# A kernel of two cross attentions and four blocks: TensorE's bursts of identity products left out, and the first attention's shift rows sent in another place of SyncE's queue

## The reference, cut to what matters

```python
x = x + xattn(ctx, ln(x), ...)          # first cross attention, no mask
x = x + selective_scan(ln(x), ...)      # state-space scan, 256 channels x 16 states
x = x + experts(ln(x), ...)             # attention of 4 heads and 8 experts + a shared one
x = x + xattn(ctx, ln(x), mask, ...)    # second cross attention, context mask
x = x + state_space(ln(x), ...)         # 4 heads, convolution of 4, state 64
x = x + fp4_block(ln(x), ...)           # weights and inputs rounded to blocks of fp4

def xattn(x, latents, mask, ...):       # x: 1601 rows, latents: 64 rows
    xn, ll = layer_norm(x), layer_norm(latents)
    q = ll @ Wq
    k, v = split(concat([xn, ll]) @ Wkv)
    weight = softmax(q @ k.T * scale)   # 16 heads of 64
    return (weight @ v) @ Wo
```

## Time and profile before

| what | value |
|---|---|
| device time, median of 3 runs | 2011.71 us (2007.66 to 2015.58) |
| the profiled execution, its own time | 2016.63 us |
| its span | 2014.9 us |
| mean granted clock of TensorE | 0.972 |
| busy: TensorE, VectorE, ScalarE, GpSimd | 94%, 82%, 63%, 46% |
| first attention's loop: its first product | at 67.68 us |
| second attention's loop: its first product | at 1104.69 us |

### The profile page before, as it was taken

The page is one execution under the profiler, slowest core; times in us unless marked ns, Lnnn a source line. Parts: engine busy times, 40 slices in busy tenths (PEclk is TensorE's granted clock), DMA queues, the critical chain, the costliest instruction groups (busy, mean ns, idle before and its releaser), DMA issues. The chain is left out here.

```text
span 2014.9 us, 34833 instructions
## 1 busy us (share of the span) xinstructions
PE 1900.2 (94%) x12250; PEld 1028.9 (51%) x12250; DVE 1646.1 (82%) x3926; ACT 1266.2 (63%) x2267; POOL 921.5 (46%) x1016
## 2 busy tenths in 40 slices
PE   7899999999999999898888999999999999998786
PEld 6444545445454545433756445454545454545584
DVE  7789899888989896599686887979797878886657
ACT  4466667676767667444234887777777777776312
POOL 5576666676667652198432533323232323232004
PEclk9899999999999999989998999999999999999898
DMA  5223222222222120132203021112111111110000
GB/s 164 70 69 89 77 80 69 69 69 69 82 69 69 53 69 2 48 118 91 83 11 82 14 48 40 39 39 61 40 39 40 43 37 44 35 31 20 12 1 11
DMA packets 148711, 110.53 MB, mean 55 GB/s; under 512 B 120876, under 2 KB 136216, under 8 KB 148408
## 3 DMA queue, kind: packets, MB, share of 16 engines
q1 hardware_dynamic: 148536, 108.31, 19.5%
HBM read 65.15 MB, written 14.29 MB: 39 GB/s over the span
## 5 line engine op out<-in xcount | busy, mean ns | idle before, releaser
L1334 DVE TENSOR_TENSOR x_p_lo<-x_psum,x_p_hi 128x512 f16<-128x512 f32 (+1 forms) x864 | 581.2, 682 | 106.5 <-ACT x_psum L1086 106.4
L1085 ACT ACTIVATE x_p_hi<-x_psum 128x512 f16<-128x512 f32 (+1 forms) x448 | 268.1, 599 | 254.2 <-PE x_psum L925 207.0
L1085 ACT ACTIVATE x_p_hi<-x_psum,x_bcol 128x512 f16<-128x512 f32 (+1 forms) x416 | 289.1, 695 | 141.2 <-PE x_psum L925 138.2
L951 PE MATMUL x_psum<-x_p_hi,x_x_both 128*128 128x512 f16 (+1 forms) x832 | 317.4, 381 | 6.5 <-DVE x_p_lo L1334 5.6
L923 PE MATMUL x_psum<-x_q,x_xT_both 128*128 128x512 f16 x832 | 316.9, 381 | 6.7 <-DMA x_q<-x_shift_rows 6.7
L924 PE MATMUL x_psum<-x_q,x_xT_both 128*128 128x512 f16 x832 | 316.3, 380 | 0.0
L925 PE MATMUL x_psum<-x_q,x_xT_both 128*128 128x512 f16 x832 | 316.3, 380 | 0.0
L952 PE MATMUL x_psum<-x_p_lo,x_x_both 128*128 128x512 f16 (+1 forms) x832 | 315.9, 380 | 0.0
L953 PE MATMUL x_psum<-x_p_hi,x_x_both 128*128 128x512 f16 (+1 forms) x832 | 315.8, 380 | 0.0
L1273 DVE CUSTOM_DVE_ANT_0 x_junk<-x_psum,x_brow 128x512 bf16<-128x512 f32 (+2 forms) x512 | 279.3, 584 | 6.5 <-PE x_psum L1002 6.3
L1276 DVE TENSOR_REDUCE x_mx<-x_psum 128x1 f32<-128x512 f32 (+2 forms) x512 | 276.4, 583 | 3.3 <-PE x_psum L1002 2.9
(11 more groups left out here) (506 smaller groups left out, 3588.0 us busy)
## 6 DMA issues: line engine op xcount, KB each, us to landing
x_x_both<-context_rows SPq DMA_DIRECT2D x32, 832.0 KB, 5.1
context_rows<-x_x SPq DMA_DIRECT2D x16, 832.0 KB, 3.4
x_raw<-in_ctx SPq DMA_DIRECT2D x16, 768.0 KB
ssm_c_row<-ssm_bc_rows SPq DMA_DIRECT2D x16, 512.0 KB, 4.6
ssm_b_wide<-ssm_bc_rows SPq DMA_DIRECT2D x7, 512.0 KB, 3.6
x_mrow<-in_mask_BxS_bk SPq DMA_DIRECT2D x16, 200.1 KB
x_xT_both<-context_rows SPq DMA_TRANSPOSE x96, 3.9
moe_W<-in_L_ffn_eW SPq DMA_DIRECT2D x3, 512.0 KB, 5.6
```

The lines of the kernel that those rows point to most:

```text
L951: pe.matmul(out, v_hi, p_hi[r][rows, :], start=start, stop=False)
L1085: act.activation(p_hi[r][rows, :], score[r][rows, :], ACT.Exp, scale=SCORE_UNIT, **bias).then_inc(p_hi_ready, 1)
L1334: v.tensor_tensor(p_lo[r][rows, :], score[r][rows, :], p_hi[r][rows, :], ALU.subtract).then_inc(p_lo_ready, 1)
```

## The change

All 21 calls of `keep_clock` are left out, and the function with them. In the first attention SyncE's queue changes in two ways. The store of batch 0 is split: `store_high` writes the high half from inside the preparation as soon as GpSimd has cast it, and the front transpose of batch 0 follows there; `store_low` writes the low half at the start of the loop's block. And for batch 1 `rows_in` stands right behind the front transpose; the other transposes, the raw rows of batch 3 and the load of batch 1 come behind it. The second attention's queue is as it was.

```diff
-def keep_clock(pe, bank, ident, n):
-    for _ in range(n):
-        pe.matmul(bank[:, 0:P], ident[:, :], ident[:, :], start=True, stop=True)
...
+        def store_high(sp):
+            sp.wait_ge(x_hi_ready, 1)
+            sp.dma_start(kept(0)[:, 0, :, :], x16[:, 0, :, :]).then_inc(high_stored, 16)
+            sp.wait_ge(high_stored, 16)
+
+        def store_low(sp):
+            sp.wait_ge(x16_ready, 1)
+            sp.dma_start(kept(0)[:, 1, :, :], x16[:, 1, :, :]).then_inc(x_stored, 16)
+            sp.wait_ge(x_stored, 16)
...
                         load_raw(sp, 1, 1, 0)
+                        store_high(sp)
+                        load_xT_front(sp, 0, 0)
...
-                    keep_clock(pe, slot_psum[3], ident, 4 if loaded else 10)
                     pe.wait_ge(fold_ready, 1)
...
                     read(pe, N_PREP - 4)
-                    keep_clock(pe, slot_of(N_PREP), ident, 4)
...
                 if not masked:
-                    store_x(sp, 0)
-                    load_xT_front(sp, 0, 0)
+                    store_low(sp)
                     load_xT_rest(sp, 0, 0)
                     load_x(sp, 0, 0)
                 rows_out(at)
...
                     load_raw(sp, 2, 0, 1)
                     store_x(sp, 1)
+                    load_xT_front(sp, 1, 1)
+                rows_in(at)
+                if not masked:
+                    load_xT_rest(sp, 1, 1)
                     load_raw(sp, 3, 1, 1)
-                    load_xT_front(sp, 1, 1)
-                    load_xT_rest(sp, 1, 1)
                     load_x(sp, 1, 1)
-                rows_in(at)
...
                 if kind == "turn":
-                    if isinstance(at, Pre):
-                        keep_clock(pe, aux[:, 512:1024], ident, 7)
                     pe.wait_ge(m_ready, at.n + 1)
...
                     aux_item(at, item)
-                keep_clock(pe, acc[0], ident, 14)
                 for u in range(AHEAD):
                     scores(u, 0, 0, 0, 0)
...
-                keep_clock(pe, slot[1], ident, 12)
                 pe.wait_ge(in_in, 16)
...
-                keep_clock(pe, slot[1], ident, 6)
                 pe.wait_ge(rest_in, 48)
...
-                keep_clock(pe, slot[1], ident, 5)
                 pe.wait_ge(fold_ready, 1)
                 pe.wait_ge(xnT_ready, 1)
...
-                keep_clock(pe, slot[3], ident, 22)
                 pe.wait_ge(heads_in, HEADS_IN)
...
-                keep_clock(pe, slot[3], ident, 5)
                 pe.wait_ge(wt_ready, 1)
                 pe.wait_ge(nxT_ready, 1)
                 product(slot[2], WT[:, Q, :], nxT, q_made)
                 product(slot[3], WT[:, K4, :], nxT, k_made)
-                keep_clock(pe, slot[0], ident, 5)
...
-                keep_clock(pe, slot[1], ident, 8)
                 pe.wait_ge(uT_ready, GROUPS)
...
-                keep_clock(pe, slot[1], ident, 12)
                 pe.wait_ge(xf_ready, 1)
...
-                keep_clock(pe, slot[1], ident, 5)
                 pe.wait_ge(xf_hi_ready, 2)
...
-                keep_clock(pe, slot[3], ident, 24)
                 pe.wait_ge(matrices_in, MATRICES_IN)
...
-                keep_clock(pe, slot[3], ident, 5)
                 pe.wait_ge(wt_ready, 3)
                 pe.wait_ge(uT_ready, 1)
...
-                keep_clock(pe, slot[3], ident, 26)
                 pe.wait_ge(yn_ready, 1)
...
-                keep_clock(pe, slot[1], ident, 10)
                 pe.wait_ge(yg_ready, 2)
...
-                keep_clock(pe, slot[3], ident, 34)
                 turn(0)
-                keep_clock(pe, slot[3], ident, 3)
                 up(0)
```

More of the change, by code:

```diff
@@ L183, in cross_attention @@
         xT_front, xT_back, xT_low = ([sem(f"{n}{k}") for k in range(2)] for n in ("xT_front", "xT_back", "xT_low"))
-        x_stored, x_hi_ready = sem("x_stored"), sem("x_hi_ready")
+        x_stored, x_hi_ready, high_stored = sem("x_stored"), sem("x_hi_ready"), sem("high_stored")
         lat_crossed = sem("lat_crossed")
@@ L606, in attention_loop @@
     if not masked:
-        load_raw, store_x, halves = held["load_raw"], held["store_x"], held["halves"]
+        load_raw, store_x, store_low, halves = held["load_raw"], held["store_x"], held["store_low"], held["halves"]
         context_mean, context_guess = held["context_mean"], held["context_guess"]
```

## The result

The median is 2022.18 us (five runs, 2021.02 to 2026.12) against 2012.78 for the kernel before (five runs, 2007.66 to 2015.58): a ratio of 1.0058 with a 95% interval from 1.0039 to 1.0077, or +9.4 us. The forecast was 2019, +7.45 to the median shown then, within a range of 2009 to 2026. A second set of the same kernel (experiment 5) gave 1.0032, from 1.0020 to 1.0043, or +6.6 us. By either the change loses more than the shift rows gain; the centre of the second lies within 0.5%, that of the first just above. One execution in experiment 6, of 3292.91 us at a granted clock of 0.586, is left out of its comparison.

The account below looks back on a forecast made before the run. TensorE, busy for 94% of the span, was taken to bound the kernel, with cold clock restarts of 2.15 us on the mean. C to J lose 13.45, B gains 6.0: +7.45 on 2011.71 gives 2019 us, range 2009 to 2026.

Parts of the forecast that it names:

- D: Start of the expert stage: twelve transposes and the products behind them run cold, +3.15 us (0 to 4.6).
- E: Ahead of the experts: transposes at half speed and first expert products cold, +2.85 us (-0.3 to 4.2).
- G: Start of the second attention's loop: cold without its burst, +2.15 us (0.5 to 3.55).
- I: End of the state-space stage: last product starts cold after a pause, +2.15 us (0 to 3.55).
- C: Start of the scan stage: transposes start earlier but slower, input products start cold, +1.85 us (-0.3 to 3.25).
- H: Start of the state-space stage: a DMA sets the late end, product behind perhaps cold, +0.5 us (-0.4 to 1.75).
- J: Last stage: four cold transposes and a longer cold stretch, +0.8 us (0.3 to 1.5).
- A and B: First attention: preparation's later clock hides behind VectorE, 0; earlier shift rows start the loop at 61.4, -6.0 us.
- F: Second attention's preparation: products start as much earlier as they run longer cold, 0, ends one restart (2.15 us) either way.
- Long restarts: Rival: cold stretches of 7.1 us instead of 4.29 at C, D, E, G and I, 2027.4 us; chance 0.20.
- Warm pauses: Rival: work before each pause keeps the clock up at C, D, E, G and I, 2008.4 us; chance 0.13.
- the rows would come no earlier: Rival: the first attention's shift rows arrive no sooner, so B is 0 and the time 2025.2 us; chance 0.05.

Follow-up runs that it names:

- experiment 5: The changed kernel once more, nothing altered: 2020.96 us (nine runs) against 2014.36 for the kernel before, ratio 1.0032.
- experiment 6: The changed kernel with bursts put back at both attention loops' starts, 2015.05 us; then also in the expert stage and at the state-space stage's end, 2009.33; before 2014.36.
- experiment 2: The kernel before with all bursts gone and SyncE's queue left as it was: 2027.38 us against 2014.82, ratio 1.0060.
- the loops' run: The changed kernel with the bursts at the two attention loops' starts put back: 2015.05 us against 2014.36 for the kernel before, ratio 1.0003.
- experiment 3: The changed kernel with the six bursts of the expert stage put back: 2012.14 us against 2014.82 for the kernel before, ratio 0.9993.
- experiment 7: GpSimd waits for VectorE in the first preparation: changed kernel 2021.31 us, changed queue with all bursts 2004.40, that with four bursts fewer 2004.27; before 2012.99.
- four places: The changed kernel with bursts back at both loops' starts, the expert stage and the state-space stage's end: 2009.33 us against 2014.36 before, ratio 0.9976.
- experiment 7's third kernel: Changed queue, GpSimd's added wait, all bursts but four (state-space stage's start, last stage): 2004.27 us, ratio 0.9950 to the kernel before.
- single transposes: The kernel before with each identity product made one transpose of the identity: 2019.10 us against 2014.82, ratio 1.0022.
- the queue's second profile: Second run of the kernel before with only SyncE's queue changed and all bursts kept: 2002.13 us against 2012.99, ratio 0.9940.
- the queue with the wait: The kernel before with the changed SyncE queue, all bursts, and GpSimd waiting for VectorE in the first preparation: 2004.40 us, ratio 0.9945.
- experiment 4: The kernel before with each identity product made one transpose, 2019.10 us against 2014.82, or two transposes, 2014.42 against 2014.36.

## Why the prediction came out as it did

The forecast of 2019 was 3 us from the first median and 2 from the second, within its range. It held as a sum of two halves: 12.6 lost against 13.45, 3.2 or 6.0 gained against 6.0 (experiment 2). That the sum of the terms came out near is in part luck: in the first profile D, E, G and I cost 3.7 us more than forecast and the middle of the state-space stage 0.8, while C, H and J cost 5.8 less. C, D and J lie outside the bounds of their own terms. The terms, one by one:

**A and B.** Right. SyncE's queue moved as worked out, the store had landed at 56.81, VectorE was the last with 59.23, the rows took 2.04 to the first product, and this began at 61.30 for a forecast of 61.4. Two misses cancel in this: the rows left at 59.26 for 58.6, and took 2.04 for 2.8. That this start is cold in both kernels was right as well, but the restart cost 1.05, not 0.3: the clock rose at 67.2 here, 5.9 us behind the first product, and at 71.4 before, 3.7 behind it, and the lag goes from -6.38 to -5.33. It was given back behind that, in a stretch that the sum didn't have: at the end of the first batch the clock fell again, from 109.0 to 115.8 before and from 104.7 to 108.1 here, and the lag is -6.57 after it. The step that failed is the cover in A: VectorE was said to hide whatever the cold front of the preparation costs. VectorE's subtraction begins at 25.83 to 26.10 in the seven profiles with the first burst and at 25.83 to 26.66 in the seven without. That is enough that in two of the six without burst and wait (the second of the changed kernel, and the loops' run) GpSimd was first and VectorE took 2.5 us or more longer. (In a third, experiment 3, GpSimd's record begins 0.01 us ahead, and it was GpSimd that took longer.) It doesn't decide the median (experiment 7).

**C.** The size was +1.85 and the first profile has -0.83, the second +1.71 (137.99 - 136.28). The products without a burst were cold in four of the profiles (7.27 to 7.59 us: changed again, bursts gone alone, loops, four places) and warm, 5.51, in three (changed, its version with the wait, bursts in experts); with a burst they took 5.50 or 5.51 in all seven. So the mechanism was right, and whether it strikes differs from execution to execution: by these seven it does in some half of them, and the term should have been some half of it.

**D and E.** Mis-sized: 5.20 and 3.57 where 3.15 and 2.85 stood. In D the products lost 2.69 (6.36 against 3.67), not 2.15: they were cold for 5.4 us (the stretch from 966.3), and half of that is 2.7, where the mean of 4.29 had stood for it. The steps behind them, which the sum had at nothing, lost another 2.1 net: there too a burst is gone, behind the products, and the stretch from 979.0 to 985.4 is cold, where the kernel before has one of 3.30. Experiment 3 confirms the two together.

**F, G, H.** 0.04, 2.44 and 0.03 for 0, 2.15 and 0.5. At H the transposes ran at half speed, but ScalarE waited for the vectors' DMA nearly as long as before, and then 0.57 for TensorE in place of 0.40; ScalarE's timeline, as the earlier trace rows:

```profile
1871.15 0.20 ACT L2353 ACTIVATE ssd_A<-ssd_A 128x4 f32<-128x4 f32 x1 [20.98 <-DMA ssd_skip<-in_L_attn_D]
...
1872.69 1.02 ACT L2358 ACTIVATE ssd_uT<-ssd_psum 128x1024 f32<-128x1024 f32 x1 [0.57 <-PE ssd_psum L2246]
```

and the product behind was warm (7.10 us before and after), as the transposes of the earlier trace rows had suggested; so it was in seven of the eight profiles without these two bursts, and 8.71 us long in the other (experiment 7's third kernel).

**I.** 2.81 for 2.15: the last product is cold for the first 5.9 of its 6.64 us, which took 3.84 before, so the mean restart was too short a measure for it.

**J.** The sign was wrong, -1.82 for +0.8. The stage takes 51.2 to 51.8 us in all eight profiles without its bursts and 51.9 to 53.3 in the five with them (51.25 with single transposes). The transposes are not held by the burst (they begin 13.43 and 13.42 us behind the stage before). At the stage's start the forecast was right: the lag grows from 7.38 to 8.34 by 2003.4, 0.96 for 0.8. The sum lacked the stage's end, the last products to the rows that are added to the latents. They were cold before and mostly warm in the changed kernel; first the stretch before, then the two of the changed kernel:

```profile
2003.40:2010.20 6.80, 5.97 (x30) 5.66 (x28) 3.11 (x4) 1.63 (x6) 3.07 (x3) 0.50 0.13 39
```

```profile
2009.40:2012.70 3.30, 3.19 (x15) 3.17 (x16) 3.16 (x5) 0.88 (x4) 2.20 (x3) 0.50 0.00 0
2012.80:2016.20 3.40, 3.33 (x27) 2.99 (x27) 1.10 (x2) 1.20 (x5) 1.07 (x2) 1.00 0.27 77
```

There the lag falls from 8.34 to 5.59. It is so in all fourteen profiles: the stage takes 53.1 to 53.3 us where its last cold stretch ends 51.6 to 51.9 us into it (before, the queue's second profile, and the queue with the wait), and 51.2 to 51.9 where that ends at 46.6 to 48.5. Why the clock came up earlier there stays open.

**The rivals.** Long restarts held at four of their five places: the cold stretches at D, E, G and I have 5.4 to 5.9 us of work in the rows above, longer than the mean of 4.29, but C and J gave back what this cost. Warm pauses held at C in three of seven profiles, and at D, E, G and I in none of those without the bursts there. That the rows would come no earlier is excluded by 61.30.

## What to carry to other kernels

Work that only keeps a clock up is not to be judged by its busy share or removed as waste: here 492 idle instructions were worth 12.6 us at a few starts, and at others nothing or less. A burst is worth something only when the real work follows it at once, so it has to be costed together with the wait that it fills: the same burst was for nothing ahead of a 6.70 us wait and worth 2.6 us when the DMA came early. Look at whether two edits of one change touch the same wait before adding their prices up.

## What the runs showed of the hardware that was not expected

Whether TensorE's clock is up at a given product can differ between two executions of one program: the scan stage's products took 5.51 and 7.58 us behind the same instructions. A restart is therefore a price with a chance, not a fixed cost.

Two subtractions on VectorE and GpSimd at the same time, both out of on-chip memory, did not run side by side: VectorE took 4.34 us for 1.63 us of work when GpSimd was 0.08 us ahead. The Trainium skill ("SBUF — State Buffer", section "SBUF: two separate sides") says of such a pair that the engine that starts first holds the shared port for the whole instruction and the other one is blocked; the two profiles of experiment 5 agree. What was not foreseen is how little decides who starts first: without the first burst VectorE began from 0.64 us ahead of GpSimd to 0.24 behind it (six profiles, without the wait); with the burst it was always 0.63 to 0.67 ahead.

A transpose of the identity keeps the clock up as a product does when it takes as long (experiment 4).
